# Two transformer layers on one core: the inverse sums and the output projection behind a projection each on TensorE, the first row maxima ahead of the division on VectorE

## The reference

```python
for l in range(2):
    h = shift_token(x)                       # second half of the channels from the token before
    q, k, v = split(h @ wqkv[l])             # 8 heads of 64
    q, k = l2norm(q) * q_scale, l2norm(k) * k_scale
    q, k = rotary_xpos(q, k)
    o = local_attention(q, k, v)             # windows of 128 tokens, each sees itself and the one before
    x = x + o @ wo[l]
    h = layernorm(shift_token(x)) * ln_g + ln_b
    a, g = split(h @ w1[l] + b1)             # 682 values and 682 gates
    x = x + (a * gelu(g)) @ w2[l] + b2
x = layernorm(x_before_the_layers + x)       # after both layers
```

## Time and profile before

| | us |
|---|---|
| median of three runs | 4105.44 (4104.93 to 4108.23) |
| the profiled execution, its own time | 4106.15 |
| its span, first to last instruction | 4104.4 |
| TensorE busy | 3928.9 (96%) |
| VectorE busy | 3043.4 (74%) |
| ScalarE busy | 2899.9 (71%) |
| GpSimd busy | 2171.0 (53%) |

### The profile page before, as it was taken

The page is one execution under the profiler, slowest core; times in us unless marked ns, Lnnn a source line. Parts: engine busy times, 40 slices in busy tenths (PEclk is TensorE's granted clock), DMA queues, the critical chain, the costliest instruction groups (busy, mean ns, idle before and its releaser), DMA issues. The chain is left out here.

```text
span 4104.4 us, 96045 instructions
## 1 busy us (share of the span) xinstructions
PE 3928.9 (96%) x36064; PEld 3297.9 (80%) x36064; DVE 3043.4 (74%) x7350; ACT 2899.9 (71%) x7339; POOL 2171.0 (53%) x2168
## 2 busy tenths in 40 slices
PE   6999999999999789999999999999999999999998
PEld 4777777777777568888888888888888888888886
DVE  4888888888888766666666666666777777777775
ACT  4777767677776567777777777777777777777775
POOL 4999999999999823333333333332333333333332
PEclk9999999999999899999999999999999999999999
DMA  7443445434453100000000000010000000000000
GB/s 118 70 71 66 71 70 78 63 66 75 72 76 56 53 25 20 15 17 20 17 15 17 20 17 15 18 33 17 22 20 30 20 25 20 30 20 25 20 25 26
DMA packets 179330, 159.26 MB, mean 39 GB/s; under 512 B 22322, under 2 KB 177844, under 8 KB 178868
## 3 DMA queue, kind: packets, MB, share of 16 engines
q1 hardware_dynamic: 177716, 152.60, 19.9%
q10 hardware_dynamic: 1152, 0.52, 0.1%
HBM read 52.40 MB, written 25.17 MB: 19 GB/s over the span
## 5 line engine op out<-in xcount | busy, mean ns | idle before, releaser
L383 ACT ACTIVATE a_p<-a_S 128x512 f32<-128x512 f32 x1024 | 528.9, 603 | 215.7 <-PE a_S L573 215.7
L279 POOL TENSOR_TENSOR a_z<-a_p 128x1024 f32<-128x1024 f32 x256 | 604.2, 2360 | 99.7 <-ACT a_p L383 95.0
L1498 PE MATMUL b_X<-b_wqkv,b_hT 128*128 128x512 f32 x2304 | 650.8, 418 | 1.3 <-DVE b_hT L1321 1.3
L1567 PE MATMUL b_F<-b_hnT,b_w 128*128 128x256 f32 (+1 forms) x4224 | 584.7, 287 | 5.8 <-issue 5.8
L1245 ACT ACTIVATE b_p<-b_S,b_nb 128x256 f32<-128x256 f32 (+1 forms) x1024 | 444.6, 446 | 160.4 <-DVE b_nb L1297 160.3
L1567 PEld LDWEIGHTS b_F<-b_hnT,b_w 128*128 128x128 f32 (+1 forms) x4224 | 533.1, 187 | 18.6 <-issue 6.2
L1498 PEld LDWEIGHTS b_X<-b_wqkv,b_hT 128*128 128x128 f32 x2304 | 418.4, 190 | 100.4 <-issue 21.8
L447 DVE TENSOR_TENSOR a_p<-a_p,a_O 128x1536 f32<-128x1536 f32 x256 | 446.7, 1745 | 4.6 <-ACT a_O L355 4.1
L1017 POOL TENSOR_TENSOR b_t<-b_t 128x512 f32<-128x512 f32 x128 | 165.5, 1293 | 529.1 <-DVE b_t L1269 529.1
L432 DVE TENSOR_REDUCE a_low_max<-a_S 128x128 f32<-128x1024 f32 x256 | 313.2, 1223 | 158.7 <-PE a_S L563 158.6
L1306 DVE TENSOR_SCALAR b_a<-b_F,w_b 128x256 f32<-128x256 f32 (+1 forms) x384 | 183.6, 478 | 293.5 <-ACT b_g L1153 290.6
(11 more groups left out here) (156 smaller groups left out, 8898.7 us busy)
## 6 DMA issues: line engine op xcount, KB each, us to landing
a_q<-a_parts SPq DMA_DIRECT2D x256, 128.0 KB, 4.9
a_k<-a_parts SPq DMA_DIRECT2D x248, 128.0 KB, 4.8
a_x<-in_x SPq DMA_DIRECT2D x16, 512.0 KB, 4.1
a_xr<-in_x SPq DMA_DIRECT2D x64, 128.0 KB, 4.8
x_after_heads<-a_n SPq DMA_DIRECT2D x64, 128.0 KB, 3.4
b_x<-x_after_heads SPq DMA_DIRECT2D x16, 512.0 KB, 4.1
x_after_layer<-b_xo SPq DMA_DIRECT2D x32, 256.0 KB, 2.3
b_x<-x_after_layer SPq DMA_DIRECT2D x16, 512.0 KB, 4.2
```

Of the source, the lines that this page charges most:

```text
L279: nc.gpsimd.tensor_tensor(z8[:], e[:, 0:8], e[:, 8:16], ALU.add).then_inc(s_zt, 1)
L383: nc.scalar.activation(probs[u % NE][:, hs], S[:, hs], ACT.Exp, scale=HDIM ** -0.5).then_inc(s_exp, 1)
L1498: last = nc.tensor.matmul(X[i][:], hT_of(k, a), wqkv[:, b, k, i * INNER:(i + 1) * INNER], start=(k == 0 and (a, b) == PART_PAIRS[0]), stop ...
L1567: last = nc.tensor.matmul(F[i % 2][0:size, part], w1[:, a, k, col:col + size], hnT[:, b, k, hf * 2 * P:(hf + 1) * 2 * P], start=(k == 0 an ...
```

## The change

On TensorE the q projection moves ahead of the spreading transposes, and the k projection ahead of the output projection, so the order after the first scores is q projection, spreading transposes, k projection, output projection. On VectorE the first row maxima move ahead of the division. No instruction is added or removed, and every wait stays with its instruction.

```diff
@@ VectorE
                 if tile_exists(T + 1):
                     low_hT(T, w_)
+                if live:
+                    row_max(T, w_, 0)
                 if tile_exists(T - 1):
                     dve.wait_ge(s_R, T)
                     nc.vector.tensor_tensor(oT[:], M[:].rearrange("p (b q) -> p b q", q=P), oU[:], ALU.mult
                                             ).then_inc(s_oTn, 1)
-                if live:
-                    row_max(T, w_, 0)
@@ TensorE
                 if live:
                     scores(T, w_, 0)
+                if tile_exists(T + 1):
+                    projection_ready(T + 1, layer(0 if w_ < 3 else 1))
+                    project(0, s_q)
                 if tile_exists(T - 1):
                     pe.wait_ge(s_rw, T)
                     pe.wait_ge(s_oU, T)
...
                     last.then_inc(s_R, 1)
                 if tile_exists(T + 1):
-                    projection_ready(T + 1, layer(0 if w_ < 3 else 1))
-                    project(0, s_q)
+                    project(1, s_k)
                 if tile_exists(T - 1):
                     pe.wait_ge(s_oTn, T)
...
                     last.then_inc(s_wo, 1)
-                if tile_exists(T + 1):
-                    project(1, s_k)
                 if live:
                     transpose_probs(T, w_, 0)
```

## The result

The changed kernel takes 4162.26 us (median of 4 runs, 4160.61 to 4163.48) against 4105.74 of the kernel before (4104.93 to 4108.23): a ratio of 1.0136, interval 1.0119 to 1.0154. It is slower by 56.5 us, where 55.8 were forecast. The profiled execution took 4161.07 us, its span 4159.3, 54.9 more than before. Of these, 52.7 lie between the first and the last tile of the layers (2593.78 us before, 2646.52 after); 1.8 lie ahead of them, in the attention part that the change does not touch.

The account below looks back on a forecast made before the run. TensorE was taken to bound most tiles, VectorE's chain first tiles of layer 2 with `final_stats`. Terms of 41.3, 6.4, 4.1 and 4 us gave 55.8 more, 4161 for the median, range 4142 to 4177 for 8 in 10.

Parts of the forecast that it names:

- The gap that changes its cause: TensorE's gap after the scores: not closed, q now waits for VectorE's `low_hT`, starting 0.04 us later than the transposes did.
- The four groups: q, transposes, k and output projection on TensorE: new sum -0.07 to +0.2 us against 4.99, taken as +0.04.
- The division: VectorE's division behind the first row maxima: costs nothing, ending half a microsecond before the output projection is due.
- The residual: VectorE's residual behind the later output projection: 1.5 us later, costing most in first and third tiles of layer 2 with `final_stats`.
- the sum: Total over all tiles: 41.3, 6.4, 4.1 and 4 us, together 55.8 on the profiled execution's 4106.15.
- The range: Bounds of the main forecast, 4148 to 4174 us; the range for 8 in 10 was 4142 to 4177.
- The three bounds: Residual and first tiles of layer 1 (-3, +5 us), the four groups (-6, +6), the first steps (-4, +3).
- Faster: Rival: the gap ahead of the spreading transposes closes and q fills it, 38.7 us less at most, 4067; chance 0.06.
- No change: Rival: VectorE's delay is swallowed everywhere, leaving about 8 us, 4113 or less; chance 0.07.
- rule of the highest occupancy: Skill's rule cited for the rivals: TensorE at 96% is the bound, VectorE at 74% has a quarter to spare.
- Slower still: Rival: the residual over 1.9 us late also eats the room of second and fourth tiles, 4188; chance 0.07.

Follow-up runs that it names:

- e6: The changed kernel with the first three matmuls of q waiting only for the first of `low_hT`'s three results: 4127.3 us, 1.0053 to the kernel before.
- e11: The kernel before with the finer wait of the q projection alone, its first half let go early: 4106.36 us, ratio 1.0.
- e8: The changed kernel with `final_stats` and the rotation of q ahead of the residual on VectorE: 4103.43 us, 0.9992 to the kernel before.
- e1: The kernel before with VectorE's part alone, first row maxima ahead of the division, TensorE's order unchanged: 4150.25 us, 1.0105.
- e3: The changed kernel with the k projection back behind the output projection; q ahead of the transposes and VectorE's part stay: 4248.28 us, 1.0346.
- e10: The kernel of e8 with the spreading transposes back ahead of q (transposes, q, k, output projection): 4095.99 us, 0.9976 to the kernel before.
- e4: The changed kernel with `final_stats` ahead of the residual on VectorE: 4114.45 us, 1.0019 to the kernel before.
- e5: The kernel before with `final_stats` ahead of the residual on VectorE: 4094.32 us, 0.9973.
- e12: The kernel of e7 with the final norm moved into VectorE's pause ahead of the third value chunk: 4063.61 us, 0.9901 to the kernel before.
- e9: The kernel of e7 with the final norm moved to the end of VectorE's step: 4093.51 us, 0.9969 to the kernel before.
- e7: The changed kernel with `final_stats` and q's rotation ahead of the residual, plus the finer wait of e6: 4067.24 us, 0.9903 to the kernel before.

## Why the prediction was right

*The gap that changes its cause.* Right: 38.7 us ahead of the transposes became 35.3 ahead of q, 123 times, released by `low_hT`. q starts 0.05 us behind VectorE's signal, as forecast from the scaling of k. e6 shows the cause, since letting half of q go early takes back 35 us; e11 shows that it was not the cause before.

*The four groups.* Mis-sized a little: 5.07 us instead of 4.99, +0.08 where I took +0.04, inside its bounds. The output projection grew, 1.54 to 1.72, as suspected, and the transposes shrank, 0.39 to 0.35. With the wait, an ordinary sequence was to lose 0.4 + 3 x 0.08 = 0.64 in layer 1; it lost 0.63. By tile this was 0.11, 0.35, 0.10 and 0.06 us, each from the start of its q transposes to the next tile's: so 0.35, the largest, lies where the first tile's late chain meets the next tile. With the rotation of q taken out of that chain (e8) it is 0.05.

*The division.* Right: it costs nothing in the changed kernel. e1 and e3 show the price without the cover, 43 and 141 us, and so that it is k's new place that covers it. The cover is smaller than half a microsecond: the weight load of the output projection is what needs the divided output, and it starts at 2395.37, ahead of its first matmul and 0.29 us behind the division's end (2394.39 + 0.69 = 2395.08).

*The residual.* Right in place and size: 1.47 us later in the tile shown and 1.53 more of waiting in the mean, 1.5 forecast. In layer 2 the first tiles lost 1.51 and the third 0.98 + 0.34 = 1.32 (the 0.44 ahead of L1599 falls into the interval of the fourth tile), where 1.5 and 1.45 stood in the sum. The second tiles won 0.08, for which the sum had 0: their gap was POOL's and shrank, as in e10. A sequence lost 2.75 instead of 2.95, and 14 of them 38.5 us instead of 41.3. The first two sequences lost 5.3 us instead of 4, the sixteen behind them 9.2 instead of 10.5. These sum to 53.0, against 52.7 measured between the first and the last tile. That the whole came to 56.5, so close to the 55.8 forecast, is in part luck: 1.8 us lie in the part ahead of the layers, and the single terms were off by 1.3 to 2.8 us in both directions.

*The range.* The three bounds were added up wrongly: 4148 takes all three at their low ends, and with two of them the bounds are 4151 and 4172. The measured time lies within these too.

*The rivals.* "Faster" failed as the rows said it would: `low_hT` ends behind the scores. "No change" failed because VectorE has no pause in these tiles. The Trainium skill's rule of the highest occupancy ("Perfetto Trace Analysis", section "Identifying the Most-Contended Engine") wants TensorE judged by its weight loads and its share of the peak rate, not by its matmul time. With weight loads for 80% of the span it still stands ahead of VectorE's 74%. In this trace that average misleads: e4, which changes nothing but the order of VectorE's work, gives back 48 us, and e5 12 us in the kernel before. "Slower still" needed a delay of 1.9 us; it was 1.5.

*What I had wrong* stands in the experiments. e1 was put at 4177 and came to 4150: the division has more room than I gave it, and tiles with 128 keys lose nothing. e5 was put at 4085 and came to 4094: second tiles of layer 2 stay long, by e12 in part for the final norm in front of the statistics, and the rest is open. e9 was put at 4061 and came to 4093, for what the norm meets on POOL. No step of the prediction had looked at either.

## What to carry to other kernels

Moving work ahead in an in-order queue delays all that it passes, and the price is paid where the consumer's own queue has no pause: read the consumer's stretch tile by tile, not its share of the span. A wait that moves onto another releaser is still a wait; make it finer, so that the first half of the work starts on the first half of its input (35 us in e6, nothing in the old order, e11). When a reorder opens a pause on another engine, fill it with work that does not need the late result: here that took back the whole loss (e8, 4103.43). Both together make the new order pay: e7 is 39 us faster than the kernel before, and 27 us faster than the old order with `final_stats` ahead (e5).

## What the runs showed of the hardware

A VectorE instruction that starts while one of POOL runs can be held until that one is done. In e9 a 128x256 scaling that began with a 1.55 us elementwise product of POOL took 1.70 us, where it takes 0.41 alone, and ended 0.15 us behind it. In 28 of the 32 pairs the second scaling did so; the first, which had begun 0.31 us before POOL's product, kept its 0.40 us. So the order of the starts decided. In the kernel before, the last pair meets such a product too: a scaling that began 0.07 us behind it took 1.61 us and again ended 0.15 behind its end. The Trainium skill, "SBUF — State Buffer", section "Who interferes with whom", says that VectorE and GpSimd share a pair of ports which one instruction holds for its whole length while the other stands fully blocked, that the one issued first gets it, and names this operation among VectorE's that can take it when its operands allow. The trace agrees in the order of the starts and in the ends, 3313.84 behind 3312.14 + 1.55 = 3313.69; it doesn't show the port itself.

From VectorE's end to the start of the weight load that waited for it, 0.05 to 0.06 us passed in the rows read for q, for the transposes of k and for the output projection. For the load of the feed-forward's last product it was 0.11 (3404.55 to 3404.66); why is not shown.
